# A second plane moved by twelve bytes, and expert outputs ordered by partition

## The reference

```python
x = x + 0.5 * _L0_ffn_ref(_layernorm(x), ...)    # mixture of 8 experts, top 2
x = x + _L0_attn_ref(_layernorm(x), ...)         # state space model (256 channels, 16 states)
x = x + 0.5 * _L0_ffn_ref(_layernorm(x), ...)    # the experts again
x = x + 0.5 * _L1_ffn_ref(_layernorm(x), ...)    # soft mixture of 64 experts, 32 slots each
x = x + _L1_attn_ref(_layernorm(x), ...)         # gated linear attention
x = x + 0.5 * _L1_ffn_ref(_layernorm(x), ...)    # the soft mixture again
```

```python
h = dA_t * h + dBu_t
y = jnp.einsum('bdn,bn->bd', h, C_t)
```

```python
gathered = out[idx_k, loc_c]
y = jnp.einsum('tk,tkd->td', gates_k * valid, gathered)
```

## Time and profile before

| | us |
|---|---|
| median of 3 runs | 2346.54 (2342.49 to 2348.29) |
| the profiled execution | 2333.07 |
| its span, from the first to the last instruction | 2331.2 |
| busy, PE / DVE / POOL / ACT | 1947.9 / 1627.1 / 1230.9 / 1034.7 |
| state scans, first to last POOL product | 383.35 to 770.61 |
| results of the experts loaded, first issue | 244.66 and 1019.24 |

### The profile page before, as it was taken

One profiled execution on the slowest core, in us unless ns is written; L12 is line 12 of the kernel. 1 busy time (PEld: TensorE's weight loads), 2 busy tenths in 40 slices (PEclk: granted clock), 3 DMA queues, 4 the chain that ended last, 5 costly groups with the idle time before them and its releaser, 6 DMA issues.

```text
span 2331.2 us, 23318 instructions
## 1 busy us (share of the span) xinstructions
PE 1947.9 (84%) x6378; PEld 958.2 (41%) x6400; DVE 1627.1 (70%) x2176; ACT 1034.7 (44%) x1548; POOL 1230.9 (53%) x775
## 2 busy tenths in 40 slices
PE   4099576888888717968999899997977999999998
PEld 3077422333333505753444344443333444444443
DVE  7133587999999822348999666674895999856554
ACT  2322286555555232225555453342444555463332
POOL 4645104999999473526999500001973999900000
PEclk9999796999999958989999999998988999999999
DMA  7122383555555022323000000002633000000000
GB/s 256 56 87 89 100 131 108 177 172 174 176 169 179 32 70 77 106 91 91 0 0 0 0 1 0 0 0 71 170 94 90 0 0 0 0 1 10 4 9 14
DMA packets 108594, 163.42 MB, mean 70 GB/s; under 512 B 11379, under 2 KB 74174, under 8 KB 108391
## 3 DMA queue, kind: packets, MB, share of 16 engines
q1 hardware_dynamic: 100326, 146.23, 21.5%
q0 software_dynamic: 8192, 16.30, 2.1%
HBM read 124.89 MB, written 38.15 MB: 70 GB/s over the span
## 4 chain that ended last, share of the span: by engine, by line
PE 53%; DVE 17%; issue 14%; POOL 11%; ACT 4%; DMA 1%; POOLq 0%; DVEq 0%; ACTq 0%; SPq 0%
PE ps L1904 10%; PE ps L1877 10%; PE ps L1636 5%; POOL arena L560 5%; PE ps L1833 5%; PE ps L1823 5%; PE ps L1646 5%; PE ps L1762 3%; DVE arena L1331 2%; POOL slot_inputs L506 2%; PE ps L1878 2%; POOL arena L539 1%; DVE arena L1497 1%; DVE stats L1055 1%; DVE stage L1080 1%
## 5 line engine op out<-in xcount | busy, mean ns | idle before, releaser
L568 POOL TENSOR_TENSOR arena<-arena 128x1024 f32<-128x1024 f32 x128 | 244.7, 1912 | 79.5 <-DVE arena L1384 74.0
L1823 PE MATMUL ps<-c_phiT,arena 128*128 128x512 f32 x512 | 266.8, 603 | 8.4 <-ACT arena L809 5.3
L1877 PE MATMUL ps<-XT,c_phiT 128*128 (+1 forms) x512 | 261.9, 593 | 0.9
L1833 PE MATMUL ps<-arena 128*128 128x512 f32 x512 | 241.2, 595 | 5.6 <-POOL arena L560 5.6
L560 POOL TENSOR_TENSOR arena<-arena 128x1024 f32<-128x1024 f32 x128 | 244.7, 1913 | 0.0
L534 POOL TENSOR_TENSOR arena<-XT,arena 128x1024 f32<-128x1024 f32 x86 | 170.0, 2000 | 140.3 <-DMA arena<-input_gates 140.3
L1904 PE MATMUL ps<-arena 128*128 128x512 f32 x512 | 226.2, 601 | 11.1 <-DVE arena L1450 11.1
L596 POOL TENSOR_TENSOR arena<-arena 128x1024 f32<-128x1024 f32 x32 | 63.6, 2000 | 310.4 <-DMA arena<-value_rows 310.3
L823 ACT ACTIVATE arena<-ps 128x1024 f32<-128x1024 f32 x128 | 131.0, 1024 | 214.7 <-PE ps L1824 214.7
L1450 DVE TENSOR_TENSOR arena<-arena 128x4096 f32<-128x4096 f32 x32 | 140.2, 4422 | 120.2 <-ACT arena L889 120.2
L882 ACT ACTIVATE arena<-ps,c_phi_bc 128x512 f32<-128x512 f32 x256 | 174.7, 687 | 90.7 <-PE ps L1878 82.8
(11 more groups left out here) (228 smaller groups left out, 3494.8 us busy)
## 6 DMA issues: line engine op xcount, KB each, us to landing
arena<-input_gates SPq DMA_DIRECT2D x128, 512.0 KB, 3.8
arena<-value_rows SPq DMA_DIRECT2D x32, 512.0 KB, 5.3
arena<-slot_inputs SPq DMA_DIRECT2D x32, 258.0 KB, 2.9
arena<-in_L_ffn_w SPq DMA_DIRECT2D x32, 256.0 KB, 3.3
arena<-token_outputs SPq DMA_DIRECT2D x16, 512.0 KB, 7.4
slot_inputs<-arena SPq DMA_DIRECT2D x1, 4128.0 KB, 13.4
slot_inputs<-zero SPq DMA_DIRECT2D x1, 4128.0 KB, 35.9
token_outputs<-arena SPq DMA_DIRECT2D x1, 4096.0 KB, 17.8
```

What stands on the lines that cost most here:

```text
L568: pool.tensor_tensor(Ed[:, r, :].rearrange("p (n q) -> p n q", q=PSLOT), Lc[:, r, :].rearrange("p (n q) -> p n q", q=PSLOT), over(mD[:, r, ...
L1823: pe.matmul(pbank(2 * h + c), xts[:, r // 2, :], phiT[:, at:at + CHUNK], start=True, stop=False)
L1833: ins = pe.matmul(pbank(4 + 2 * h + c), xns[:, r // 2, :], Dd[:, r, CHUNK * c:CHUNK * (c + 1)], start=start, stop=stop, skip_group_check=True)
L1877: pe.matmul(pbank(t % 4), phiT[:, P * t:P * (t + 1)], xt(b, c), start=True, stop=False)
```

## The change

The change has two parts that are independent of each other.

First, `Cs`. The second plane of the output gate no longer lies in row 3 of `XT` from its word 1 on, but right behind the first plane. The first plane stays where it was.

Second, the order of the rows in `token_outputs`. The result of the token at tile t and partition p gets row 2 x (32 p + t) + choice in place of 2 x (128 t + p) + choice. The numbers that travel with the rows change with it, and so does the pattern of the loads back: a group of four tiles is, for each partition, 8 rows of 512 bytes one after the other, 4 KB in one piece, where it was four pieces of 1 KB.

```diff
@@ -225,7 +225,8 @@
         dtu = XT[:, 0:2, CONV_PAD:]
-        Cs = XT[:, 2:4, 1:1 + TIME]
+        Cs = XT[:, :, :].rearrange("p b t -> p (b t)")[:, 2 * (CONV_PAD + TIME) + 1:2 * (CONV_PAD + TIME) + 1 + 2 * TIME]\
+            .rearrange("p (a t) -> p a t", t=TIME)
         Bs = cut([NB, TIME])
@@ -426,7 +427,7 @@
-                yv = ytok[m].rearrange("(t p q) d -> p t q d", p=P, q=K)
+                yv = ytok[m].rearrange("(p t q) d -> p t q d", p=P, q=K)
@@ -2071,7 +2072,7 @@
-        "k_row_id": (K * np.arange(TOKENS).reshape(TILES, P).T + 1).astype(f),
+        "k_row_id": (K * np.arange(TOKENS).reshape(P, TILES) + 1).astype(f),
```

## The result

| | before | changed |
|---|---|---|
| median of 4 runs, us | 2345.75 (2342.49 to 2348.29) | 2358.32 (2355.28 to 2359.59) |
| ratio, 95% interval | | 1.0052 [1.0035, 1.0070] |
| span of the profiled execution, us | 2331.2 | 2353.4 |
| first to last start of a POOL product in the scans, us | 383.35 to 768.61, 385.26 | 391.96 to 788.07, 396.11 |
| `token_outputs`, first load to landing, first and second pass, us | 3.93, 3.88 | 3.72, 3.86 |

The changed kernel is 12.6 us slower, where 10.5 were forecast, and its median is 1.3 us above the 2357.0 of the forecast. One line was added to the kernel's text, so line 534 of before is 535 now, 539 is 540, and so on.

What follows compares the result with a forecast made beforehand. POOL, busy 386.59 of 387.26 us, was taken to bound the scan stage. +10.9 us (planes) and -0.4 us (row order) gave +10.5 on the 2346.54 us median: 2357.0 us, range 2345 to 2363.

Steps and rivals of the forecast that it cites:

- POOL is the bound of the stage: Scan stage: POOL busy 386.59 of 387.26 us, so any change in its products moves the stage's end by as much.
- The plane that moves is the fast one and becomes slow: Output products, line 539: plane 1 goes from remainder 2 to 7 by eight, from 2.00 to 2.35 us.
- The size: Output products of the scans: 0.35 us more for each of 32 on plane 1, 11.2 us of work.
- 31 of 32 count: End of the scans: the last slowed product is hidden by PE's sum, so 10.9 of 11.2 us count.
- ACT's copy to the new address: Gate copies in the scans: could grow by 0.35 us before POOL waits.
- Part two: Return of expert rows: two first loads land 0.25 and 0.20 us earlier, about -0.4 us, between -2.0 and +1.4.
- The end at 0: Loads of `token_outputs`: gain may be 0, since input-gate loads have a median of 3.8 us.
- only the first load is on the path: Loads of `token_outputs`: in each pass only the first of eight is waited for; the other seven land ahead of need.
- Seven is the only slow remainder: POOL products: by eights of words, 7 is the only remainder slow in the trace, and both planes will have it.
- The rule weighed against: POOL products: about 2.6 cycles an element whatever the address, so the first part would cost nothing.
- The rival built on it: Scans: address does not decide, line 539 keeps two speeds, only the row order counts; 2346.1 us, chance 0.10.
- The 13.5 us between before's profile and its median: Whole kernel: three runs' median 2346.54 us lies 13.5 above the profiled 2333.07; carried over to the forecast.

Runs made afterwards that it cites:

- The opposite test: Kernel before with output gate plane 0 moved to 2058 words, plane 1 kept at 3082, old row order: 2321.06 beside 2331.46 us, ratio 0.9954.
- part one alone: Kernel before with only the second output gate plane moved right behind the first, old row order: 2343.04 beside 2331.46 us, ratio 1.0047.
- the repetition: The changed kernel, both parts, run again on a third chip against the kernel before: 2343.08 beside 2333.00 us, ratio 1.0043.
- all four kernels profiled: Kernel before with gate planes, step-size planes or attention buffers at other offsets, one with only attention buffers moved: 2344.32, 2360.02, 2392.41, 2342.74 beside 2342.91 us.

## Why the prediction was right

- **POOL is the bound of the stage.** Shown: 11.5 us more of work on POOL (398.07 against 386.59) lengthened the way from first to last start by 10.85 us, forecast 10.9, and left POOL's one wait at 0.4 us. The opposite test shows how near the next bound is: with 11 us less work, POOL waited 1.5 us more for DVE.
- **The plane that moves is the fast one and becomes slow.** Shown by the 64 products at 2336 ns and more, and by the reverse with all at 2.00 us. The step that carried it was to assign the slow products to a plane by the order of g, and not to trust the word "equal" in either direction.
- **The size.** Forecast 0.35 us a product; the shortest product went from 1986 to 2336 ns, 0.35. The starts are 6.22 us apart, forecast 6.21. The busy time of the 64 products is 151.9 us where 150.6 were forecast. That is not a longer way: the recorded durations reach past the next start and differ between executions (means of 2.36, 2.37 and 2.38 us in the three profiles with both planes moved), while the starts are 6.22 us apart in all three, so the step between starts is the safer measure.
- **31 of 32 count.** The last product's growth was hidden under PE's sum of the term before, as the same 1.48 us between their starts shows.
- **ACT's copy to the new address** costs nothing: 204.31 against 204.27 us of ACT in the stage.
- **Part two.** Forecast -0.4 us; the profiles give -0.5 on the path, and neither end of its bounds came near (the scatter's landing did not move at all). The end at 0 stood on the input gates' median of 3.8 us; the first loads in the new order took 3.44 to 3.86. The forecast said nothing of the stream's rate, which rose from 354 to 399 GB/s. It made no difference because only the first load is on the path, as the forecast had it.
- **Where the forecast was too coarse.** "Seven is the only slow remainder" held for the rows at hand and for the place that the change uses, but the period is four words, not eight. A plane at remainder 3 would have been forecast as fast, from the input product's 3 words: there the *first* operand stands at 3, which is a difference of 5. The forecast did not ask which operand was which.
- **The rule weighed against.** The price of 2.6 cycles an element from the "GPSIMD Engine Reference" of the Trainium skill has no address in it; the measured products of one form differ by 17.5% (2350 against 2000 ns) by their address alone. The rival built on it (2346.1 us) lies outside of what was measured.
- **The last 2 us.** 12.6 us were measured first, 10.5 forecast, 11.6 for part one alone and 10.1 in the repetition. The intervals (for the first one 8.2 to 16.4 us) hold all of these, so nothing remains to be explained. The 13.5 us between before's profile and its median, which the forecast carried over without a reason, are of the size by which before differs between the chips (2331 to 2333 us against 2343 to 2346), so the profile and the median were probably taken on different ones. That is argued, not shown; the difference between the kernels does not rest on it.

## What to carry to other kernels

Where one form of instruction shows two durations in strict alternation, find the loop variable that has the same period, and compute the addresses of both operands before an edit makes them "equal": the fast one may be the one that moves. Two tensors that GpSimd multiplies are worth placing with a deliberate difference of 1 or 2 words by four, as soon as GpSimd is the bound; here moving one plane by three words was worth 0.4%. A DMA that becomes faster in the middle of a queue gains nothing while only its first load is waited for.

## What the runs showed of the hardware

- A GpSimd product of two float32 SBUF operands of 128 x 1024 took 2.00 us (medians 1.99 to 2.04) where the second operand's start was 1 or 2 words behind the first's by four, and 2.35 us (2.34 to 2.38) where it was 0 or 3; for 128 x 512 the medians were 1.09 us (difference 2 or 1) and 1.26 to 1.27 us (7 or 0).
- Loads of 512 KB in 128 pieces of 4 KB streamed at 399 to 401 GB/s in the first passes, in 512 pieces of 1 KB at 347 to 354. SP's issue of eight of them took 3.8 to 4.0 us in place of 7.1 to 7.2.
- Indirect writes of 128 rows of 512 bytes landed after 2.20 to 2.25 us, whether the rows were near each other or 32 KB apart.
- On one chip all four kernels profiled had a stop of 10.9 us in the waits of DVE at the first routing, and on two others none of six. The kernel before took 2343 us on the first and 2331 and 2333 on the others. In the comparison at the head, where it took 2346 us, the changed kernel has the stop as well, and its ratio, 1.0052, agrees with the 1.0043 of the repetition. A profile and a median that may come from two chips must not be subtracted.
